# Conv attention block on one core: opening fillers 17 to 4 + 2, gate weight copy moved, transposed probabilities copied by two engines

## The reference

```python
xn   = layernorm_over_W(x);  q, k, v = conv3x3(conv1x1(xn))          # 8 heads of 4 channels
probs = softmax(k^T q / scale)                                        # 4 x 4 per head, over 1024 pixels
x1   = conv1x1(v @ probs) + x
xn   = layernorm_over_W(x1)
x2   = conv1x1(gelu(conv3x3(conv1x1(xn))) * conv3x3(conv1x1(xn))) + x1   # gate * info, 64 channels
h    = leaky_relu(instance_norm(conv3x3(x2)))
mask = sigmoid(conv3x3(h));  xm = h * mask;  out1 = conv3x3(h)
out2 = local attention of xm, each pixel over its 3 x 3 neighbours    # softmax of 9 scores
y    = x2 + out1 * mask + (1 - mask) * out2
```

## Time and profile before

| | |
|---|---|
| time, median of 3 runs (lowest to highest) | 206.95 us (206.83 to 207.28) |
| profiled execution: its own time | 208.39 us |
| profiled execution: span from first to last instruction | 206.6 us |
| busy: TensorE, VectorE, ScalarE, GpSimd | 176.9, 153.5, 106.3, 71.1 us |
| chain that ended last, shares of the span | TensorE 55%, VectorE 22%, ScalarE 7%, DMA 4% |

### The profile page before, as it was taken

The page is one execution under the profiler, slowest core; times in us unless marked ns, Lnnn a source line. Parts: engine busy times, 40 slices in busy tenths (PEclk is TensorE's granted clock), DMA queues, the critical chain, the costliest instruction groups (busy, mean ns, idle before and its releaser), DMA issues.

```text
span 206.6 us, 7256 instructions
## 1 busy us (share of the span) xinstructions
PE 176.9 (86%) x3151; PEld 119.5 (58%) x3161; DVE 153.5 (74%) x362; ACT 106.3 (51%) x192; POOL 71.1 (34%) x60
## 2 busy tenths in 40 slices
PE   1599979989768999999877999999889698999980
PEld 1557627748363846687454556787437245666750
DVE  6895499948694878699596994894747876993762
ACT  2282563313780452635994721648614884955650
POOL 8600630550005403480005651751403013670480
PEclk9999999999978999999999999999999999999999
DMA  5521004000240001001000031000000000000002
GB/s 187 107 63 54 2 25 127 3 10 3 75 118 19 0 8 17 3 3 41 3 0 3 0 105 22 3 6 13 32 24 8 0 3 10 5 8 8 3 0 105
DMA packets 11312, 6.34 MB, mean 31 GB/s; under 512 B 9168, under 2 KB 9648, under 8 KB 11280
## 3 DMA queue, kind: packets, MB, share of 16 engines
q1 hardware_dynamic: 11040, 5.29, 10.0%
q10 hardware_dynamic: 240, 0.58, 0.8%
HBM read 3.35 MB, written 1.05 MB: 21 GB/s over the span
## 4 chain that ended last, share of the span: by engine, by line
PE 55%; DVE 22%; ACT 7%; issue 6%; DMA 4%; SPq 3%; POOL 1%; DVEq 0%; ACTq 0%
PE ps L1474 9%; PE ps L1376 9%; PE ps L1435 6%; PE ps L1349 5%; PE ps L1342 5%; PE ps L1386 4%; DVE sh_in L326 3%; DMA w3b<-in_w_gi 3%; SPq L395 2%; PE ps L1509 2%; PE ps L1498 2%; PE ps L1334 2%; PE ps L1537 2%; DVE prob L1192 2%; DVE sh_x L326 2%
## 5 line engine op out<-in xcount | busy, mean ns | idle before, releaser
L483 POOL TENSOR_TENSOR ln_s<-ln_s,neg_half 128x16 f32<-128x16 f32 x7 | 20.3, 2907 | 63.1 <-DVE ln_s L940 63.1
L1435 PE MATMUL ps<-ln_out,w_gi 32*64 32x256 f32 x1152 | 33.6, 377 | 1.2 <-DVE x L1082 0.8
L1435 PEld LDWEIGHTS ps<-ln_out,w_gi 32*64 32x64 f32 x1152 | 25.6, 130 | 7.2 <-issue 2.4
L1376 PE MATMUL ps<-w_qk,sh_ln 128*128 128x128 f32 x192 | 24.9, 290 | 4.5 <-DMA sh_ln<-ln_out 3.2
L1376 PEld LDWEIGHTS ps<-w_qk,sh_ln 128*128 128x128 f32 x192 | 23.8, 204 | 5.9 <-issue 4.9
L1474 PE MATMUL ps<-sh_in,w_in 96*32 96x256 f32 x384 | 22.5, 381 | 1.9 <-DVE sh_in L326 1.9
L1342 PE MATMUL ps<-busy 128*128 128x512 bf16 x69 | 18.8, 402 | 1.4 <-issue 1.3
L1474 PEld LDWEIGHTS ps<-sh_in,w_in 96*32 96x32 f32 x384 | 11.6, 110 | 11.5 <-DVE sh_in L326 2.8
L618 ACT ACTIVATE sh_ln<-ln_out 32x512 f32<-32x512 f32 (+1 forms) x29 | 15.2, 524 | 5.2 <-DVE ln_out L918 4.8
L618 ACT ACTIVATE sh_x<-x 32x496 f32<-32x496 f32 (+1 forms) x20 | 12.3, 616 | 3.3 <-DVE x L1082 2.8
L618 ACT ACTIVATE sh_in<-act_c 32x496 f32<-32x496 f32 (+1 forms) x20 | 12.3, 617 | 3.2 <-DVE act_c L1140 2.9
(11 more groups left out here) (142 smaller groups left out, 337.1 us busy)
## 6 DMA issues: line engine op xcount, KB each, us to landing
x_res<-in_x SPq DMA_DIRECT2D x4, 256.0 KB, 2.7
out_x<-out_s SPq DMA_DIRECT2D x4, 256.0 KB, 2.8
sh_ln<-ln_out SPq DMA_DIRECT2D x15, 64.0 KB, 2.1
x_norm<-in_x SPq DMA_DIRECT2D x3, 256.0 KB, 2.9
kc<-in_shape_consts ACTq DMA_DIRECT2D x1, 450.0 KB, 4.8
w3b<-in_w_gi SPq DMA_DIRECT2D x1, 288.0 KB, 5.5
x_norm<-in_x SPq DMA_DIRECT2D x2, 128.0 KB, 2.8
ln_out<-ln_out SPq DMA_DIRECT2D x8, 25.5 KB, 2.4
```

What stands on the lines that cost most here:

```text
L483: nc.gpsimd.tensor_tensor(ln_s[n][:, 3, :], ln_s[n][:, 2, :], neg_half[:, :], ALU.pow)\
L1376: mm = nc.tensor.matmul(to, sh_ln1[pair % 2][:, d, i, WD * y:WD * y + P], w_qk[:, dy, :, :, :].rearrange("p d m c -> p (d m c)"), start=(d ...
L1435: mm = nc.tensor.matmul(ps[EC * i:EC * i + EC, r, BLK * m:BLK * m + BLK], w_gi[rows, dx, m, dy, :], src[rows, i, dy:dy + RH, dx:dx + W], s ...
```

## The change

It has three parts. The opening has 4 fillers and no wait for the first image's norm steps in place of 12 + 5 fillers, and 2 new fillers between the two `qk` products. `gate_info_folds()` stands ahead of `qk_t_evac(0, 1)` on ScalarE instead of behind it. `probs_t` on ScalarE copies only the lower 64 partitions, in all pairs, and `probs_t` on VectorE copies the upper 64: in step 0 between the shift and the neighbour copies of norm 1 of pair 3, in step 1 behind `ln2_apply`, for pair 2 in the tail behind `window_softmax` of pair 3. `window_out` and `conv1` wait for both engines' signals.

```diff
-        g_t_sb = signal("probs_t_in_sbuf", [4] * (PAIRS - 1) + [2], start=1)
-        g_t_dve = signal("last_probs_t_in_sbuf", [0] * (PAIRS - 1) + [2])
+        g_t_sb = signal("probs_t_in_sbuf", 2, start=1)
+        g_t_dve = signal("probs_t_in_sbuf_by_dve", 2, start=1)
...
                 for t in range(2):
                     act.wait_ge(g_t.sem, g_t.at(pair, t + 1))
-                    for h in range(1 if early else 2):
-                        rows = slice(KSLOT * h, KSLOT * h + KSLOT)
-                        nc.scalar.activation(p_t[rows, 4 * R * t:4 * R * t + 4 * R, h, :],
-                                             ps[rows, values_banks(early)[t], :].rearrange("p (q m) -> p q m", m=TH * TW),
-                                             ACT.Copy).then_inc(g_t_sb.sem, 1)
+                    nc.scalar.activation(p_t[0:KSLOT, 4 * R * t:4 * R * t + 4 * R, 0, :],
+                                         ps[0:KSLOT, values_banks(early)[t], :].rearrange("p (q m) -> p q m", m=TH * TW),
+                                         ACT.Copy).then_inc(g_t_sb.sem, 1)
...
             qk_t_evac(0, 0)
             squares(0, 1)
+            gate_info_folds()
             qk_t_evac(0, 1)
-            gate_info_folds()
             head_exp(0)
...
-            def last_probs_t(pair):
+            def probs_t(pair, early=False):
...
                 if norm:
-                    ln1_apply(pair + 3)
+                    ln_apply(0, ln1_out, "ln1", pair + 3)
                 else:
                     ln2_apply(pair + 2)
+                probs_t(pair)
+                if norm:
+                    ln1_neighbours(pair + 3)
+                    planes("ln1", ln1_out, sh_ln1, g_ln[0], g_v4, pair + 3)
                 gated(pair + 1)
...
             window_softmax(last, True)
+            probs_t(but_last)
             window_probs(last)
-            last_probs_t(last)
+            probs_t(last, True)
             final(last)
...
             def conv1(pair, early=False):
                 if not early:
                     pe.wait_ge(g_t_sb.sem, g_t_sb.before(pair))
+                    pe.wait_ge(g_t_dve.sem, g_t_dve.before(pair))
...
                     if t % (UNITS // 4) == 0:
-                        pe.wait_ge(g_t_sb.sem, g_t_sb.at(pair, (half + 1) * (1 if early else 2)))
-                        if early:
-                            pe.wait_ge(g_t_dve.sem, g_t_dve.at(pair, half + 1))
+                        pe.wait_ge(g_t_sb.sem, g_t_sb.at(pair, half + 1))
+                        pe.wait_ge(g_t_dve.sem, g_t_dve.at(pair, half + 1))
...
             pe.wait_ge(s_busy, 1)
-            stay_busy(12, 5)
-            pe.wait_ge(g_im[0].sem, g_im[0].done(0))
-            stay_busy(5, 5)
+            stay_busy(4, 5)
             pe.wait_ge(s_wready, W_QKV)
             qk(0, 0)
+            stay_busy(2, 5)
             qk(0, 1)
```

More of the change, by code:

```diff
@@ L1201, in last_probs_t @@
                     nc.vector.tensor_copy(p_t[KSLOT:P, 4 * R * t:4 * R * t + 4 * R, 1, :],
-                                          ps[KSLOT:P, values_banks(True)[t], :].rearrange("p (q m) -> p q m", m=TH * TW))\
+                                          ps[KSLOT:P, values_banks(early)[t], :].rearrange("p (q m) -> p q m", m=TH * TW))\
                       .then_inc(g_t_dve.sem, 1)
```

## The result

| | before | after |
|---|---|---|
| executions timed side by side on one chip | 22 | 22 |
| median (lowest to highest), us | 206.96 (205.47 to 209.75) | 205.32 (203.82 to 207.61) |
| profiled execution: its own time, and span | 208.39, 206.6 | 205.06, 203.2 |

The ratio is 0.994, with an interval of 0.991 to 0.997: 1.2 us of gain (0.7 to 1.8) where 2.8 were forecast. It leaves out the most disturbed executions, five of before and one of after; with them the medians lie 1.64 us apart. The sign was right and the time lies in the range, but the size was not.

What follows compares the result with a forecast made beforehand. The opening was taken as bound by an unbroken chain of waits through TensorE's fillers, the first product, GpSimd's roots and VectorE. Terms -2.5 - 0.2 - 0.2 + 0.1 = -2.8 took 206.95 to 204.1 us, range 202.3 to 206.0.

Steps and rivals of the forecast that it cites:

- Rival (c): Clock drop at 59.64 falls away as the idle stretch before it shifts: 1.7 us more gained, 202.4 us; chance 0.10.
- the added drop: The same shift of the idle stretch could add a clock drop elsewhere: 206 us; chance 0.05.
- The opening: Fewer fillers ahead of the first `qk` product, two before the second, weight copies moved at no cost: 2.5 us gained.
- (a): In the opening TensorE's clock rises only behind the first product, so almost no gain there: 206.4 us; chance 0.10.
- (b): In the opening the clock stays at 1.2 GHz through the second product too: slower, 210.5 us; chance 0.07.
- The weight copies' cover: In the opening, ScalarE's moved gate weight copies end 0.6 us ahead of the second product's end, so cost nothing.
- Step 0: ScalarE loses two probability copies and gelu starts 0.8 us earlier, VectorE pays; 0.2 us gained, bounds +0.5 and -0.7.
- Step 1: VectorE does its probability copies in idle time, gelu can start at 144.0 instead of 144.18: 0.2 us gained.
- The tail: VectorE's copies for pair 2 start its sums 0.2 us later; cost between 0 and 0.2, taken as 0.1 us.
- (d): The opening's gain holds but VectorE's copies cost more, through step 0: 204.6 to 205.2 us; chance 0.13.

Runs made afterwards that it cites:

- e4: Changed kernel with ScalarE's first squares moved ahead of its wait for the vectors' load and its exp table load; ratio 0.992, mean 205.03 us.
- e10: Kernel before plus ten fillers at TensorE's wait for pair 2's planes, three before step 0's second reduce product, four behind step 1's `conv1`; ratio 1.000, mean 206.15 us.
- e6: Changed kernel plus ten fillers where TensorE waits for pair 2's planes; ratio 0.990 against the kernel before.
- e3: Kernel before with only the copies of the transposed probabilities split between ScalarE and VectorE, old opening kept; ratio 0.999.
- e2: Kernel before with only the opening changed: 4 + 2 fillers and gate weight copies moved earlier; ratio 0.995, mean 205.43 us.
- e8: Kernel before with the split probability copies and ten fillers where TensorE waits for pair 2's planes; ratio 0.993, mean 205.28 us.
- e5: Kernel before plus ten fillers where TensorE waits for pair 2's planes; ratio 0.995, mean 205.76 us.
- e7: Changed kernel plus ten fillers at TensorE's wait for pair 2's planes, three before step 0's second reduce product, four behind step 1's `conv1`; ratio 0.983, mean 203.44 us.
- e11: The e7 kernel timed again on another chip; ratio 0.987 against the kernel before, mean 203.28 us.
- e9: Kernel before with only the opening changed, plus ten fillers where TensorE waits for pair 2's planes; ratio 0.988, mean 203.46 us.
- e1: Kernel before timed once more with nothing edited; ratio 0.998, mean 207.01 us.
- e12: The e7 kernel with the gate weight copies put back behind the second product's copy; ratio 0.986 against the kernel before, mean 203.70 us.

## Why the prediction was right or wrong

**The step that failed** is the one behind the sum: "I take the difference over to the median". It holds only if what differs between executions of one kernel is the same in both kernels. The drop is not. Where fillers keep it away (but for two of 36 executions), after is 2.6 us faster than before, and the sum said 2.8. Unfilled, before takes 206.63 - 205.95 = 0.7 us more than filled (44 of 93 executions at 1.27 make 0.6), and after takes 205.46 - 203.36 = 2.1 more, give or take 0.6, having the drop in every execution. So the gain was made, and about half of it (1.4 of 2.6) was given back, for the most part at a place that the change does not touch.

These three differences add up to the measured 1.2 by the way they are formed, so the sum confirms nothing; what shows the cause is that the full gain is there when the stretches are filled. They are means over several chips, each uncertain by 0.2 to 0.5. One drop, 3.41 us at half the clock, can cost 1.7 directly; the 2.1 is above that, within its scatter. Without fillers there is one reading, a thin one: the two executions of e4 without a drop took 204.05, which is 2.0 less than the 49 of before without one.

The prediction had the mechanism and mis-sized it. Rival (c) said that the idle stretch shifts against the moments at which the clock changes; it gave the loss of the drop a chance of 0.10 and an added one 0.05, at 1.7 us each, where a drop in before goes with 1.3. The one profiled execution of before has a drop, and I took that for a property of the kernel; then a shift could only remove it. The hint was there: the profiled 208.39 lies 1.4 us above the median of the three times, which is about one drop. Rival (c)'s second half, the added drop, came nearest to what happened.

Also mis-sized was the bound of what a measurement can tell: 0.2%, 0.4 us, from three runs. The 93 executions of before lie between 204.8 and 209.5.

**The opening** (-2.5): right. The table gives, for six traces, the clock's rise (read off the spacing of fillers or `qk` products, as in the prediction) and the start of `gate_info(0)`, both in us after the first filler.

| | rise | `gate_info(0)` |
|---|---|---|
| before, opening of 17 | 2.65 | 31.32 |
| after, opening of 4 + 2 | 2.68 | 28.80 |
| before with both filled (e10) | 4.68 | 32.33 |
| after with the stretch filled (e6) | 4.68 | 29.66 |
| the probabilities alone (e3) | 5.27 | 32.63 |
| the opening alone (e2) | 5.29 | 29.94 |

The column's first two rows are these lines, of before and of after (first fillers at 12.62 and 13.06):

```profile
43.94 1.56 PE L1435 MATMUL ps<-ln_out,w_gi 32*64 32x256 f32 x48 [0.38 <-ACT v L639]
41.86 1.56 PE L1438 MATMUL ps<-ln_out,w_gi 32*64 32x256 f32 x48 [0.47 <-ACT v L639]
```

At an equal rise the new opening is 2.5 to 2.7 us shorter, early or late. This settles (a) and (b): the rise does come up to 2.6 us later in some executions, but in both kernels, so the difference stays; and in none of the traces did the second product run at the lower clock. The paths fell as worked out: the forecast had the first product end 4.88 us behind the first filler and it was 5.00, the second at 8.08 and it was 8.13, the roots at 10.2 and they were 10.2. `ln_scale` follows `head_scores`, as said. The weight copies' cover was forecast at 0.6 and was 0.72.

**Step 0** (-0.2, bounds +0.5 and -0.7): right in its steps. Counted from the start of `gate_info(1)`, gelu came 0.7 us earlier (0.8 forecast), `gated` 0.6 later (0.7 forecast), `inorm` follows `ln_var`, and came 0.44 earlier, more than the 0.2 forecast. What I did not look for was what these shifts do to TensorE: its waits grew to 1.10 us (0.51 in before) and 1.46 us (1.16), and behind the second of them e3 and e4 have a second drop. With the stretch filled (e8 against e5) the probabilities are worth 0.5 us in all, but next to the new opening (e7 and e11, 203.36, against e9, 203.46) only 0.1. Neither can be told from the 0.3 forecast, nor from nothing.

**Step 1** (-0.2): wrong, it gained nothing. gelu started 0.13 us earlier, but VectorE did not follow at once. The chain of waits of after:

```profile
140.96 0.61 ACT gate L658
...
141.62 0.40 issue
142.02 0.70 DVE gi L1072
...
148.41 1.88 PE ps L1352 x13
```

Between gelu's first half and `gated` lie 0.40 us in which VectorE waited for nothing that the profile shows. It is no accident of one execution: from gelu's start to that of `gated` it is 1.05 or 1.06 us in all eight traces with the new copies, and 0.70 in all six with the old. Why is open. It takes more than the gain, and `conv1` starts 17.41 us behind `gate_info(2)` where it was 17.37.

**The tail** (+0.1, between 0 and 0.2): at the lower bound. From ScalarE's copy of `out1` to the end of VectorE's last instruction both kernels take the same, 10.40 and 10.41 us. The timeline of after, for the earlier trace rows:

```profile
189.99 1.30 DVE L1199 COPY p_t<-ps 64x512 f32<-64x512 f32 x2
191.33 0.65 DVE L1186 TENSOR_REDUCE wsm<-prob 128x8 f32<-128x480 f32 x1
191.77 1.10 PE L1568 MATMUL ps<-p_t,v_t 128*32 128x64 f32 x64
192.02 1.27 POOL L517 TENSOR_TENSOR dif<-omm,out 128x512 f32<-128x512 f32 x1
192.25 1.55 DVE L1190 TENSOR_TENSOR prob<-prob,wsm 128x480 f32<-128x480 f32 x1
```

The normalisation (L1190) took 1.55 us instead of 1.66 and ended 0.51 us behind GpSimd's product in both kernels: VectorE came later and was held for less. The rule of the Trainium skill (SBUF — State Buffer, Who interferes with whom) gave 0, and the trace agrees with it. (d) fell with this: VectorE's copies took 0.69 us each, as the earlier trace rows had them, and TensorE's idle time ahead of the four `window_out` is 1.4 us in both kernels, none of it waiting for a copy.

Of the 3.4 us between the profiled spans 3.05 are there when the tail begins (`out1` copied at 193.06 and 190.01). The rest lies in the last transfer out: from the end of VectorE's last instruction to the end of the span it is 3.14 us in before and 2.78 in after, where the change does nothing.

**Open**: why the earlier start makes the drop nearly certain. Six traces hold the stretch unfilled. The length of the idle time is a rival that they do not exclude: 2.49 (e4), 2.71 (e3 and after), 3.18 (e2) and 3.23 us (before) came with a drop, 2.43 (e1) without. But the new opening does not make it longer: it is 2.49 to 3.18 with the new opening and 2.43 to 3.23 with the old. What the new opening does move is its place: counted from the clock's first rise it begins at 36.4 (e2), 37.3 (e4) and 37.8 us (after), and with the old opening at 39.1 (e3), 40.2 (e1) and 40.4 (before). That its place decides fits best, but no run here moved the stretch alone by known steps, so it is argued and not shown. Three of 24 executions of the changed kernel with both stretches filled (e7, e11, e12) still had a drop, at times no longer than the others'; no profile caught one, and its place is open.

## What to carry to other kernels

A drop of the clock in one profiled execution is a sample: before a profile's difference is carried over to a median, look at the granted clock of every timed execution, and forecast separately for those with a drop and those without. Work removed far ahead of a stretch in which TensorE is idle can change how often the clock falls behind it, so the stretch belongs into the sum. A few products that nobody reads are better spent there than in the opening: the changed kernel with both stretches filled takes 203.4 us, faster than both kernels here. The opening alone with ten fillers in one stretch (e9, 203.5) does as well, without the new copies.

## What the runs showed of the hardware

- The clock's fall behind an idle stretch differs from execution to execution of the same program: in 44 of 93 of before, in 44 of 46 with the shorter opening and nothing filled, in 1 of 36 with ten fillers in the stretch and the old opening (e5, e8, e10). One such fall goes with 1.3 us more in before (207.28 against 206.01). In the kernels with the shorter opening it goes with 0.7 in e4 (204.70 against 204.05, two of them without) and 1.4 in e6 (205.24 against 203.88, two without); the changed kernel unfilled and with both stretches filled differ by 2.1.
- The first rise came between 2.2 and 5.3 us after the first filler in fourteen traces, whichever the opening was, and the opening's end moves by about half of that. It does not show in the clock column, which reads 1.00 from the start, but in the spacing of the fillers.
- ScalarE and VectorE read the two halves of one PSUM bank's partitions at the same time (92.71 and 92.72 above) without a loss to VectorE: its two copies took 1.30 us there, and 1.30 at 189.99, where ScalarE read another bank.
